# z_in rows by TensorE products, five segments instead of four, and GpSimd four quads behind the ranking

## What is computed

```python
edge_index = jnp.stack([src, dst])
h = jnp.maximum(_layernorm(x, axis=-1), 0.0)
in_deg  = jnp.minimum(segment_sum(ones, dst), 511)
out_deg = jnp.minimum(segment_sum(ones, src), 511)
sum3d = segment_sum(edge_attr @ W_sum + b_sum, src)
x = x + h + z_in[in_deg] + z_out[out_deg] + sigmoid(cent @ W_cent + b_cent) \
      + sigmoid(vor @ W_vor + b_vor) + sum3d
```

## Time and profile before

| | |
|---|---|
| time, median of 3 runs | 2475.61 us (2472.15 to 2476.04) |
| time of the profiled execution | 2477.0 us |
| its span, first to last instruction | 2475.2 us |
| mean granted TensorE clock, share of full speed | 0.770 |
| POOL busy | 1852.2 us (75%), x1869 |
| DVE busy | 1655.5 us (67%), x5321 |
| PE busy | 1568.7 us (63%), x8689 |
| ACT busy | 895.0 us (36%), x4489 |
| DMA | 451.90 MB, mean 183 GB/s |

### The profile page before, as it was taken

The page is one execution under the profiler, slowest core; times in us unless marked ns, Lnnn a source line. Parts: engine busy times, 40 slices in busy tenths (PEclk is TensorE's granted clock), DMA queues, the critical chain, the costliest instruction groups (busy, mean ns, idle before and its releaser), DMA issues.

```text
span 2475.2 us, 40112 instructions
## 1 busy us (share of the span) xinstructions
PE 1568.7 (63%) x8689; PEld 1168.9 (47%) x8689; DVE 1655.5 (67%) x5321; ACT 895.0 (36%) x4489; POOL 1852.2 (75%) x1869
## 2 busy tenths in 40 slices
PE   5756666666666432237766765666677766687776
PEld 2234554444454210016555554554565655566655
DVE  8946677878878621549887754444576665698766
ACT  3533333444343533545444433333233333001323
POOL 5777777777777777777777777777777777766786
PEclk7867667766766555559988888777799888899888
DMA  5356544445555553348767776666688777799996
GB/s 141 99 157 197 152 130 129 135 142 158 153 154 156 153 175 106 105 122 234 213 206 213 207 214 187 189 181 183 207 257 236 234 229 216 192 243 222 243 249 187
DMA packets 485071, 451.90 MB, mean 183 GB/s; under 512 B 72407, under 2 KB 444637, under 8 KB 484828
## 3 DMA queue, kind: packets, MB, share of 16 engines
q1 hardware_dynamic: 402782, 300.08, 45.0%
q0 software_dynamic: 78752, 136.44, 17.5%
q10 hardware_dynamic: 3294, 12.80, 1.6%
HBM read 319.28 MB, written 129.59 MB: 181 GB/s over the span
## 4 chain that ended last, share of the span: by engine, by line
POOL 51%; DMA 19%; issue 19%; DVE 4%; PE 3%; ACT 2%; DVEq 1%; SPq 1%; ACTq 0%; POOLq 0%
POOL sorted L528 51%; DMA edge_ring<-in_edge_attr_dram 6%; DMA sorted<-edge_ring,pos_i 6%; DMA edge_ring<-in_L_gnn_z_out_dram,out_i 5%; DMA piece_ring<-sorted 2%; PE bank L1011 2%; ACT junk L863 1%; DVE acc L712 1%; DVE hot_n L685 1%; PE bank L1030 1%; DVE base L800 0%; SPq L423 0%; PE bank L957 0%; DVE gate_normed L751 0%; ACT edge_ring L878 0%
## 5 line engine op out<-in xcount | busy, mean ns | idle before, releaser
L528 POOL DMA_INDIRECT sorted<-edge_ring,pos_i x1660 | 1604.0, 966 | 524.9 <-issue 487.4
L1011 PE MATMUL bank<-piece_ring,hot_n 128*125 128x129 f32 x4920 | 860.6, 326 | 210.3 <-DVE hot_n L685 186.3
L1011 PEld LDWEIGHTS bank<-piece_ring,hot_n 128*125 128x125 f32 x4920 | 772.4, 227 | 348.8 <-DVE hot_n L685 306.3
L685 DVE SCALAR_TENSOR_TENSOR hot_n<-bank,wkey,piece_ring 128x250 f32<-128x250 f32 x1230 | 579.4, 471 | 509.6 <-DMA piece_ring<-sorted 484.6
L863 ACT ACTIVATE junk<-bank,mark_col 128x100 bf16<-128x100 f32 x1664 | 543.4, 337 | 142.9 <-PE bank L988 141.8
L994 PE MATMUL bank<-hot_w,after_b 128*128 128x400 bf16 x416 | 177.6, 427 | 573.6 <-ACT junk L863 568.6
L878 ACT ACTIVATE edge_ring<-key_f 128x5 f32<-128x5 f32 x332 | 69.6, 210 | 1093.3 <-DMA edge_ring<-in_edge_attr_dram 1092.4
L712 DVE TENSOR_TENSOR acc<-bank,acc 125x129 f32 x1230 | 348.3, 283 | 42.5 <-issue 26.5
L994 PEld LDWEIGHTS bank<-hot_w,after_b 128*128 128x128 bf16 x416 | 45.8, 110 | 643.5 <-ACT junk L863 643.3
L863 ACT ACTIVATION_READ_ACCUMULATOR junk<-bank,mark_col 128x1 f32 x1664 | 334.1, 201 | 0.0
L1037 PE MATMUL bank<-hot_dl,hot_dh 128*125 128x100 bf16 x1661 | 199.9, 277 | 27.7 <-DVE hot_dh L620 25.6
(11 more groups left out here) (109 smaller groups left out, 1182.5 us busy)
## 6 DMA issues: line engine op xcount, KB each, us to landing
piece_ring<-sorted SPq DMA_DIRECT2D x1230, 130.0 KB
edge_ring<-in_edge_attr_dram SPq DMA_DIRECT2D x332, 320.0 KB
sorted<-edge_ring,pos_i POOLq DMA_INDIRECT x1660
base<-in_x_dram SPq DMA_DIRECT2D x20, 560.0 KB
out_dram<-base ACTq DMA_DIRECT2D x19, 560.0 KB
out_dram<-base SPq DMA_DIRECT2D x9, 560.0 KB
base<-out_dram SPq DMA_DIRECT2D x9, 560.0 KB
edge_ring<-in_L_gnn_z_out_dram,out_i POOLq DMA_INDIRECT x100, 6.8
```

The costliest lines, as they stand in the source:

```text
L528: g.indirect_dma_start(rows, bass.IndirectOffsetOnAxis(index, 0), edge_ring[:, slot, at, :], None).then_inc(s_scatter[slot], 16)
L685: v.scalar_tensor_tensor(out=hot_n[:, n % HOT_SLOTS, 0:G, :], in0=iota_ps.unsqueeze(1).to_broadcast([P, G, LOC]), scalar=wkey[:, s % 2, c: ...
L1011: last = t_.matmul(to, hot_n[:, n % HOT_SLOTS, k, :], piece_ring[:, n % PIECE_SLOTS, k, 0:SUM], start=(k == 0), stop=(k == ROW_GROUPS[s] - 1))
```

## The change

Three things change.

1. **z_in rows on PE.** The in-degrees stay as floats (`deg_f`). Once the histogram is done SP loads the whole table `z_in` into the place of `dst_parts` (`z_table`, four blocks of 128 rows). For each window PE spreads the 125 degrees over the partitions by a product with a one-hot (`look(k, 0)`), DVE compares them with the row numbers (`hot_z`, 128x500), PE sums four products of 128x125 by 128x256 (`look(k, 1)`), and DVE adds the result to the node row. The planner puts these 200 half steps into `side[q]` from quad 161 to quad 409. POOL's 100 `z_in` gathers and DVE's 100 adds in the tail are gone. `guests_out` now waits for this add (`s_z_in`), and the five batches of `stats` replace two.
2. **Segments** of 25, 165, 110, 70 and 46 quads instead of 25, 185, 130 and 76. Pieces go from 150 + 470 + 360 + 250 to 150 + 430 + 320 + 240 + 190. The tail has 190 steps with `ahead` = 90 instead of 250 with 150.
3. **POOL's wait.** From quad 8 on POOL begins quad q only once PE has done `rank(q + 4)`.

```diff
-SEGMENT_QUADS = (25, 185, 130, 76)
-ROW_GROUPS = (2, 2, 2, 2)
+SEGMENT_QUADS = (25, 165, 110, 70, 46)
+ROW_GROUPS = (2, 2, 2, 2, 2)
...
-GUEST_GATHERS = 18
-GUEST_LEAD = 12
+TABLE_LEAD = 4
 INDEX_RING = 8
+RANK_LEAD = 4
...
@@ the planner
-        for line in ("hist", "node"):
+        for line in ("hist", "node", "look"):
...
+                if kind == "look" and (todo["hist"] or q < look_quad or b >= nodes):
+                    break
...
@@ SP
-                sp.wait_ge(s_node, (i + 1) * X_WINDOWS)
+                sp.wait_ge(s_z_in, (i + 1) * X_WINDOWS)
...
+                if q == table_quad:
+                    sp.wait_ge(s_count, count_signals(NQ - 1))
+                    sp.dma_start(z_table, z_in.rearrange("(c p) d -> p c d", p=P)).then_inc(s_table_in, 16)
@@ POOL
                 pool.wait_ge(s_index, q + 1)
+                if q >= 2 * RANK_LEAD:
+                    pool.wait_ge(s_rank, min(q + RANK_LEAD, NQ))
...
-            for kind, w in z_order:
...
+            for w in range(NW):
+                pool.wait_ge(s_out_deg, w // COUNTED + 1)
+                if w >= GATHERS:
+                    pool.wait_ge(s_added, added["z_out", w - GATHERS])
+                g.indirect_dma_start(z_rows[0:NODE_P, w % GATHERS, :], None, z_out[:, :],
+                                     bass.IndirectOffsetOnAxis(out_i[0:NODE_P, w:w + 1], 0)
+                                     ).then_inc(s_z_row[w % GATHERS], 16)
@@ DVE
+            def look(k, late):
+                if late:
+                    row = base[0:NODE_P, order[k] % ROW_SLOTS, :]
+                    dve.wait_ge(s_look, k + 1)
+                    dve.wait_ge(s_node, k + 1)
+                    v.tensor_tensor(row, ps_look[k], row, ALU.add).then_inc(s_z_in, 1)
+                else:
+                    dve.wait_ge(s_spread, k + 1)
+                    v.tensor_tensor(hot_z[:, k % 2, :, :], ps_degree[k].unsqueeze(1).to_broadcast([P, KZ, LOC]),
+                                    row_z[:, :].unsqueeze(2).to_broadcast([P, KZ, LOC]), ALU.is_equal).then_inc(s_hot_z, 1)
@@ PE, called in each quad between rank(q) and the rest of side[q]
+            def look(k, late):
+                if k == 0 and not late:
+                    pe.wait_ge(s_in_deg, 1)
+                    pe.wait_ge(s_table_in, 16)
+                if late:
+                    pe.wait_ge(s_hot_z, k + 1)
+                    for c in range(KZ):
+                        last = t_.matmul(ps_look[k], hot_z[:, k % 2, c, :], z_table[:, c, :], start=(c == 0), stop=(c == KZ - 1))
+                    last.then_inc(s_look, 1)
+                else:
+                    before = [j for j in range(k) if look_bank[j] == look_bank[k]]
+                    if before:
+                        pe.wait_ge(s_z_in, before[-1] + 1)
+                    t_.matmul(ps_degree[k], deg_f[0:NODE_P, order[k]:order[k] + 1].to_broadcast([NODE_P, P]),
+                              ident[0:NODE_P, 0:LOC], start=True, stop=True).then_inc(s_spread, 1)
```

More of the change, by code:

```diff
@@ L138, in gnn_kernel @@
                      + [(0, ("node", j, (j > j0) + 2 * (j < j1))) for j in range(j0, j1 + 1)]],
+            "look": [(0, ("look", k, late)) for k in range(NW) for late in range(2)],
             "stats": [(0, ("stats", j, 0)) for j in range(NW)]}
@@ L204, in gnn_kernel @@
     ahead = pieces[NS - 1] - SW
-    tail_adds = sorted([(4 + w * (ahead + 20) // ROW_SLOTS if w < ROW_SLOTS
-                         else ahead + BACK_LAG + (w - ROW_SLOTS) * (NW - BACK_LAG - 5) // GUESTS, "z_in", w) for w in range(NW)]
-                       + [(ahead + ADD_LAG + w, "product", w) for w in range(NW)]
+    tail_adds = sorted([(ahead + ADD_LAG + w, "product", w) for w in range(NW)]
                        + [(ahead + Z_LAG + w, "z_out", w) for w in range(NW)])
     added = {(kind, w): n + 1 for n, (_, kind, w) in enumerate(tail_adds)}
[L211 to L216, removed]
     store_start = list(range(0, SW - STORE_WINDOWS + 1, STORE_WINDOWS)) + [SW - 2, SW]
@@ L300, in gnn_kernel @@
         ps_y = bank[6:8]
+        ps_degree = [bank[look_bank[k]][:, D:D + LOC] for k in range(NW)]
+        ps_look = [bank[look_bank[k]][0:NODE_P, 0:D] for k in range(NW)]
         ps_gate = bank[7][0:NODE_P, 0:2 * D]
@@ L312, in gnn_kernel @@
         s_piece_in = [sem(f"s_piece_in{i}") for i in range(PIECE_SLOTS)]
-        s_z_row = ([sem(f"s_z_row{i}") for i in range(GATHERS)], [sem(f"s_z_guest{i}") for i in range(GUEST_GATHERS)])
+        s_z_row = [sem(f"s_z_row{i}") for i in range(GATHERS)]
+        s_table_in = sem("s_table_in")
+        s_spread = sem("s_spread")
+        s_hot_z = sem("s_hot_z")
+        s_look = sem("s_look")
+        s_z_in = sem("s_z_in")
         s_out = [sem(f"s_out{i}") for i in range(REST_PARTS)]
@@ L586, in _ @@
             v.tensor_copy(iota_ps, iota_n[:, 0:LOC])
+            for c in range(KZ):
+                v.tensor_scalar(row_z[:, c:c + 1], pid[:, :], float(c * P), None, ALU.add)
             dve.wait_ge(s_made, 3)
@@ L789, in add_to_row @@
                     dve.wait_ge(s_guest[(w - ROW_SLOTS) // X_WINDOWS], 64)
-                before = [added[kind_, w] for kind_ in ("z_in", "product", "z_out") if added[kind_, w] < added[kind, w]]
+                before = [added[kind_, w] for kind_ in ("product", "z_out") if added[kind_, w] < added[kind, w]]
                 if before:
@@ L796, in add_to_row @@
                 else:
-                    ring, n, _ = ring_of[kind, w]
-                    places = z_places[ring]
-                    dve.wait_ge(s_z_row[ring][n % len(places)], 16 * (n // len(places) + 1))
-                    last = v.tensor_tensor(row, places[n % len(places)][0:NODE_P, :], row, ALU.add)
+                    dve.wait_ge(s_z_row[w % GATHERS], 16 * (w // GATHERS + 1))
+                    last = v.tensor_tensor(row, z_rows[0:NODE_P, w % GATHERS, :], row, ALU.add)
                 last.then_inc(s_added, 1)
@@ L837, in _ @@
                         piece(s, i)
-            dve.wait_ge(s_node, NW)
+                for what, k, late in side[q]:
+                    if what == "look":
+                        look(k, late)
+            dve.wait_ge(s_z_in, NW)
             for c in range(pieces[NS - 1] + Z_LAG):
@@ L1007, in piece @@
                     if s == 1 and c == 0:
-                        pe.wait_ge(s_in_deg, 1)
+                        pe.wait_ge(s_z_in, max(k for k in range(NW) if look_bank[k] == 5) + 1)
                 to = piece_sums(s, c)
@@ L1055, in _ @@
                 rebase(q)
-            pe.wait_ge(s_in_deg, 1)
-            pe.wait_ge(s_node, NW)
+            pe.wait_ge(s_z_in, NW)
             for b in range(2):
```

64 lines of the change are left out of this document (30 added, 34 removed).

## The result

The change takes 2399.24 us (median of 4 runs, 2396.79 to 2400.55) against 2473.88 for the kernel before on the same chip (2470.49 to 2476.04). The ratio is 0.9695, with a 95% interval of 0.9683 to 0.9706: 3.05% faster, 74.6 us. Forecast were 2428 us, 47.6 us less than before, and a range of 2380 to 2485; the measured time lies inside the range and just under the 2400 to 2450 that the forecast itself was given. The profiled execution took 2399.9 us, its span is 2398.0.

The account below looks back on a forecast made before the run. The prediction took POOL, full with scatters until 2132 us, to bound the kernel, with the tail behind it. Span 2475.2 - 87 (tail) + 40 (POOL's wait), looks charged nothing, gave 2428 us; range 2380 to 2485.

Parts of the forecast that it names:

- POOL is the bound of the quad loop and the tail adds to it: Quad loop: POOL is full until 2132 us, one scatter per 1.271 us; the tail of 342.4 us lies behind it.
- Part 1: Tail: without POOL's 100 z_in gathers and DVE's 100 adds, and with 60 fewer steps, 255 us for 342.4, gain 87.
- 4.6 + 60 + 173 + 17: Tail from POOL's end: 4.6 to first piece, 90 steps of 0.66, 99 of 1.75, 17 for last steps and stores.
- two reasons given for it, the first: Tail's last 99 steps: a z_out gather needs 1.2 + 7.1 + 0.3 = 8.6 us over five steps, 1.72 a step.
- The second reason: Tail's last 99 steps: a step moves 447 KB through the DMA engines, at 262 GB/s 1.71 us.
- The prediction's split: Tail's gain of 87 us: about 49 from the 60 steps the last segment loses, the rest from the gathers.
- Part 2: Quad loop, quads 161 to 409: looks and 100 more pieces fit on DVE and PE; charged 0, 31 us in the range.
- The 78 and 80 scatters: Two 100 us stretches before: 78 scatters with DVE busy 89.8 us, 80 with 70.2; read as at most 2.5% POOL loss.
- Part 3: Quad loop: POOL's wait for the rank stops it at start, quad 28 and boundaries 190, 300, 370; 40 us, bounds 20 and 75.
- PE at the low clock: Rival, quads 161 to 196: PE stays at 1.2 GHz and sets the pace, 7.0 us a quad, 2495 us; chance 0.12.
- The quick rival: Quad loop and tail: wait nearly free, stalls of 20 us, tail of 233 at POOL's pace, 2386 us; chance 0.16.
- Landing times: Slow-landing rival, tail's second stretch: landing rises to 12.3 us, steps stay at 2.0 us, 25 us more, 2453; chance 0.14.

Follow-up runs that it names:

- the first four runs: The change without POOL's wait, 2382.71 us; with one rank more, 2421.1 us; with the four segments of before, 2436.3 us; the kernel before with five segments, 2455.17 us.

## Why the prediction was right, and where it was off

- **POOL is the bound of the quad loop and the tail adds to it.** Right on the first kind of chip: with the wait removed there is no gap over 0.4 us in the loop, and every stop of the change is in the total.
- **Part 1, the tail.** Forecast 4.6 + 60 + 173 + 17 = 255, measured 4.6 + 57.9 + 165.4 + 18.9 = 246.8. The gain is 95.6 us, not 87. The mis-sized term is the last 99 steps, 1.67 us for 1.75. Of the two reasons given for it, the first was added up wrongly: the 7.1 us to landing of the earlier trace rows is counted from the start of POOL's instruction, so it holds the 1.2 us already, and the way of a gather is 7.1 + 0.3 = 7.4 us, 1.48 a step and not 1.72. It doesn't set the pace on the slower chips, where eight steps go no faster than five; on the first kind DVE still waits 37.7 us for gathers, and no run there gave it more steps. The second reason, the DMA engines with 1.71 us a step, is not shown and not refuted; that 1.75 came near is in part luck. The first 90 steps came as read from the earlier trace rows, 0.643 for 0.66.
- **What part brings what.** From the first four runs: segments alone 20 us; looks with four segments and the wait 39 us, and 55 with the 16 us added by which the last scatter comes later. Both, without the wait, 93. The rest, 17 us by the medians and 13 by the spans of the profiled executions, is their meeting: fewer steps gain little while POOL's gathers fill the tail. The prediction's split (49 us for the 60 steps, the rest for the gathers) is not what the runs show: the five segments bring 37 us once the looks are there and 20 without them.
- **Part 2, looks at no charge.** Right on this kind of chip: apart from the five stops no gap in the loop is over 0.4 us. A look costs PE 74.6 / 32 = 2.3 us for its four products (2.5 taken) and 13.0 / 32 = 0.4 for the spreading, which the prediction left out; DVE's compare takes 0.668 us. The loss of up to 31 us that the prediction allowed for by the rule of the Trainium skill on the shared port pair (SBUF — State Buffer, section "SBUF: two separate sides") did not come: a scatter takes 967 ns on average where it took 966, 1 us in all. The 78 and 80 scatters that it was read from say nothing of DVE: at 1.271 us a scatter 100 us hold 78.7, so the count depends on where a stretch is cut.
- **Part 3, the wait. This is the step that failed.** The stops were priced as the ends of `rank(q + 4)`, but the counter is reached by `rank(q + 3)`. The section on the change has the same slip in its third point. Priced 40 us, measured 17.4: 3.8 us at quad 8 became nothing, 6.5 at 28 became 1.7 at 29, and 10, 9 and 9 at the boundaries became 4.0 and 0.6, 6.3, and 4.7. The rank before it had ended earlier at each of these places. In the trace of before the 217th starts at 1104.3 and is over before quad 213 is ready at 1107.4; the 218th holds up only the next quad, ready at 1112.5, and the stop is 1118.5 - 1112.5 = 6.0 us instead of 11.1. The run with one rank more has the price that was forecast, 40 us: its last scatter is 40.1 us later than before's.
- **The rivals.** PE at the low clock did not come: 0.85 and 0.81 from 800 to 1000 us. The quick rival, 2386, lies 13 us from the measured time and the forecast 29: its stalls of 20 us are nearly what came (17.4), while its tail of 233 at POOL's pace was not reached (246.8). Landing times did not rise, 7.0 for 7.1 us.
- The number was inside the range although one of its two terms was priced at more than twice what it measured. The two misses point the same way, so neither hides the other: the last scatter came 18.4 us later where 40 were forecast, 21.6 less, and the tail is 8.2 us shorter than 255. That is the 30 us between spans of 2428 and 2398.

## What to carry to other kernels

Count what a semaphore stands at before pricing a wait on it: one increment more or less was over half of the stops here (22 of 40 us), since each stop is the difference of two large times. A wait put on the engine that is the bound cost its late cases here, 17 us, however free it was in the steady stretches. And time such a wait on more than one chip: on the slower ones it saves 87 to 90 us in the kernel before, and 137 in the change with Z_LAG 12.

## What had not been expected of the hardware

The same program takes 2474 to 2475 us where the change and the first four experiments ran, and about 3000 us on three other chips, with little spread on each (2990 to 3016 in their runs). The traces of the slower ones show the same duration of a scatter (median 958 to 962 ns, as 958), but signals that arrive late: from PE's `rank` to ACT up to 14.2 us without the wait and 11.5 with it, over 1 us in 184 to 203 of 416 quads, against at most 0.2 us on the first kind. In 154 of 185 cases in the kernel before with the wait, and in 189 of 203 with Z_LAG 12, they arrive between one scatter's end and the next one's start, though such gaps are only 36 and 37% of the loop. That POOL's unbroken issue of indirect DMAs holds such signals back fits this, and fits that a wait which makes POOL stop sooner saves 137 us.

The reverse must be weighed too: POOL stops because it waits for such a signal, so the two would fall together in any case. The times speak against it. In these two traces the middle half of the late signals that fall into a stop of POOL (a gap over 0.4 us) arrives 1.4 to 1.8 us after the stop began, while the stop itself began anywhere from 2.2 to 4.7 us (again the middle half) after the rank had ended and ACT was free to take it. So the arrival keeps time with POOL's stop and not with PE's rank. It is still argued from these times, not shown, as no run changed the length of POOL's stops by itself. Why the chips differ stays open.
